# The second normalisation of a two-layer graph network: transposes and scores from fp16 halves, in another order

## The reference

```python
h = relu(layernorm(x))                              # layer 0
x = x + (adj != 0) @ (h @ W0 + b0) / deg[:, None]    # deg: column sums of adj != 0

h = relu(layernorm(x))                              # layer 1, the second normalisation
ht = (h @ W1) split into 4 heads of 512
src, dst = ht . a_src, ht . a_dst                   # one score per node and head
e = leaky_relu(src[i] + dst[j], 0.01) + adj[i, j]
x = x + mean over heads of softmax(e, over j) @ ht
```

## Time and profile before

| | us |
|---|---|
| median of three runs | 2477.36 (2476.27 to 2477.75) |
| profiled execution | 2477.34 |
| its span | 2475.5 |
| TensorE busy in the span | 2451.6 (99%) |
| VectorE, ScalarE busy | 1873.6 (76%), 1259.9 (51%) |
| layer 0 up to its last block | to 350.03 |
| last block with the second normalisation | 350.03 to 428.92 |
| hand-over to layer 1's first matmul | 428.92 to 441.94 |

### The profile page before, as it was taken

One profiled execution on the slowest core, in us unless ns is written; L12 is line 12 of the kernel. 1 busy time (PEld: TensorE's weight loads), 2 busy tenths in 40 slices (PEclk: granted clock), 3 DMA queues, 4 the chain that ended last, 5 costly groups with the idle time before them and its releaser, 6 DMA issues.

```text
span 2475.5 us, 42808 instructions
## 1 busy us (share of the span) xinstructions
PE 2451.6 (99%) x12355; PEld 1199.9 (48%) x12355; DVE 1873.6 (76%) x2575; ACT 1259.9 (51%) x1886; POOL 47.8 (2%) x44
## 2 busy tenths in 40 slices
PE   7999999999999999999999999999999999999999
PEld 4444446444444444444444444444444444444787
DVE  7788767976688676887768876687776887667786
ACT  4645546744455444554445544455445554444554
POOL 0000000000000000000000000000000000000000
PEclk9999999999999999999999999999999999999999
DMA  4276747100121001210012000121000300001000
GB/s 149 98 273 187 246 154 224 60 3 5 43 81 37 1 5 34 89 35 4 5 34 89 35 4 5 34 89 35 4 5 27 96 34 3 3 13 49 26 1 10
DMA packets 74079, 143.95 MB, mean 58 GB/s; under 512 B 4473, under 2 KB 11899, under 8 KB 72826
## 3 DMA queue, kind: packets, MB, share of 16 engines
q1 hardware_dynamic: 73978, 142.82, 18.0%
HBM read 129.11 MB, written 13.70 MB: 58 GB/s over the span
## 4 chain that ended last, share of the span: by engine, by line
PE 83%; issue 10%; DVE 5%; DMA 1%; ACT 1%; POOL 0%; DVEq 0%; POOLq 0%; ACTq 0%
PE z_ps L776 70%; PE o_ps L804 11%; DVE hl_reg L977 2%; DMA ring_reg<-adjT_in 1%; PE o_ps L1428 1%; PE c_ps L1428 1%; DVE z_reg L993 0%; DVE ao_reg L990 0%; ACT h_reg L1251 0%; DVE w_reg L1075 0%; DVE t_reg L968 0%; PE o_ps L1413 0%; ACT w_reg L1258 0%; PE c_ps L790 0%; DVE hl_reg L968 0%
## 5 line engine op out<-in xcount | busy, mean ns | idle before, releaser
L776 PE MATMUL z_ps<-hl_reg,h_reg 128*128 (+2 forms) x8712 | 1752.0, 364 | 1.3 <-DVE hl_reg L635 1.3
L776 PEld LDWEIGHTS z_ps<-hl_reg,h_reg 128*128 (+1 forms) x8712 | 852.4, 98 | 897.6 <-issue 2.3
L574 ACT ACTIVATE hl_reg<-t_reg (+2 forms) x363 | 360.7, 994 | 722.3 <-DVE t_reg L663 379.2
L635 DVE TENSOR_TENSOR hl_reg<-t_reg,hl_reg (+2 forms) x363 | 416.5, 1147 | 229.3 <-ACT hl_reg L574 226.9
L559 ACT ACTIVATE t_reg<-ring_reg,vv 128x512 f32 (+3 forms) x726 | 524.8, 770 | 66.3 <-DVE ao_reg L650 60.9
L663 DVE SCALAR_TENSOR_TENSOR t_reg<-t_reg,vv,e_reg (+3 forms) x728 | 510.5, 743 | 8.5 <-issue 8.0
L650 DVE TENSOR_TENSOR ao_reg<-ao_reg,t_reg 128x1024 f32<-128x1024 f32 (+1 forms) x336 | 383.8, 1142 | 0.0
L804 PE MATMUL o_ps<-w_reg,z_reg 128*128 128x512 f16 x1248 | 278.2, 379 | 0.9 <-DVE z_reg L679 0.9
L804 PEld LDWEIGHTS o_ps<-w_reg,z_reg 128*128 128x128 f16 x1248 | 119.8, 98 | 140.9 <-DVE z_reg L679 1.2
L679 DVE SCALAR_TENSOR_TENSOR z_reg<-z_ps,z_reg 128x512 f16<-128x512 f32 (+1 forms) x112 | 73.2, 654 | 151.5 <-ACT z_reg L586 151.5
L463 ACT ACTIVATE e_reg<-e_reg (+2 forms) x91 | 90.5, 995 | 152.7 <-DVE e_reg L474 152.7
(11 more groups left out here) (178 smaller groups left out, 1094.8 us busy)
## 6 DMA issues: line engine op xcount, KB each, us to landing
ring_reg<-adjT_in SPq DMA_DIRECT2D x78, 512.0 KB, 4.5
e_reg<-adjT_in SPq DMA_DIRECT2D x78, 512.0 KB, 3.6
ring_reg<-x_in SPq DMA_DIRECT2D x13, 512.0 KB, 4.1
x_dram<-ring_reg SPq DMA_DIRECT2D x13, 512.0 KB, 5.0
ao_reg<-x_dram SPq DMA_DIRECT2D x6, 1024.0 KB, 5.6
out_dram<-ao_reg SPq DMA_DIRECT2D x6, 1024.0 KB, 4.5
ring_reg<-c_dram SPq DMA_DIRECT2D x23, 256.0 KB, 3.3
h_reg<-x_in SPq DMA_DIRECT2D x3, 1536.0 KB, 15.8
```

The costliest lines, as they stand in the source:

```text
L574: nc.scalar.activation(hl_ring[:, g % HL_RING, 0, :, 0:W], t_ring[:, g % T_RING, :, 0:W], ACT.Copy).then_inc(hi_ready, 1)
L635: nc.vector.tensor_tensor(hl_ring[:, g % HL_RING, 1, :, 0:W], t_ring[:, g % T_RING, :, 0:W], hl_ring[:, g % HL_RING, 0, :, 0:W], ALU.subtr ...
L776: mm = nc.tensor.matmul(z_ps[:, k, 0:W], hk[hs], hl_ring[:, r, ps, u, 0:W], start=first and u == 0 and n == 0, stop=last and u == 1 and n ...
```

## The change

For all tiles but the last, the fp16 halves in `h16` are transposed instead of the fp32 stage: eight fp16 transposes per tile into the same bank, one copy of 1024 fp16 elements to `ht1_16`, and four times two matmuls with `wa16`, the two fp16 halves of `wa` side by side (16 columns). The eight columns of each half are added by VectorE at the end (`sdc`). A transpose now waits for the pair's low half. The scores of a tile come one step after the transposes of the next. Steps and maxima are placed anew. The first four pairs are loaded early into `ln1_stage` itself and are normalised there in place; the sums of eight tiles run in the last eleven turns of `awork`. The halves of tiles 20 to 22 go to `late_h`, a part of `ao_reg`, and are moved to `h16` by a DMA after the late steps, for which TensorE waits after the first 24 matmuls of layer 1. In VectorE's groups splits are put between the sums, ScalarE's order is written out, and the variances of the last group but one come ahead of the remaining splits and row maxima.

```diff
-        LN1_AT = [math.ceil(6 + 5 * m / 3) for m in range(NT - 1)]
+        LN1_AT = [math.ceil(5 + 1.9 * m) for m in range(NT - 1)]
-        LATE_MAX_AT = [4, 10, 16]
-        MR_AT = 24
+        LATE_MAX_AT = [4, 17, 27]
+        MR_AT = 36
+        SUM_G = LAST0 + 2
...
                 def transpose1(i):
-                    pe.wait_ge(st1_ready, i + 1)
+                    t = tiles1[i]
+                    if i == 0:
+                        pe.wait_ge(o_sb, o_count(NB - 1))
                     if i >= 2:
                         pe.wait_ge(tr_sb, i - 1)
-                    for k in range(KT):
-                        mm = nc.tensor.transpose(o_ps[:, i % 2, k * P:(k + 1) * P],
-                                                 ln1_stage[:, (i // 2) % 2, i % 2, k * P:(k + 1) * P], ident[:])
+                    if i < NT - 1:
+                        pe.wait_ge(st1_split, unit(i) + 1)
+                        pe.wait_ge(s_i16, 1)
+                        h = late_h[:, t - L0] if L0 <= t < L0 + 3 else h16[:, t]
+                        for s in range(2):
+                            for k in range(KT):
+                                mm = nc.tensor.transpose(o16[:, i % 2, (s * KT + k) * P:(s * KT + k + 1) * P],
+                                                         h[:, s, k * P:(k + 1) * P], ident16)
...
                 def scores(i):
...
                     for k in range(KT):
-                        mm = nc.tensor.matmul(c_ps[:, t * 2 * H:(t + 1) * 2 * H], ht1[:, i % 2, k], wa3[:, k],
-                                              start=k == 0, stop=k == KT - 1)
+                        if i < NT - 1:
+                            for s in range(2):
+                                mm = nc.tensor.matmul(c_ps[:, t * 4 * H:(t + 1) * 4 * H], ht1_16[:, i % 2, s, k],
+                                                      wa16[:, k].rearrange("p s r -> p (s r)"),
+                                                      start=k == 0 and s == 0, stop=k == KT - 1 and s == 1)
...
                         if step == LN1_AT[i]:
                             transpose1(i)
-                            if i > 0:
-                                scores(i - 1)
+                        if i > 0 and step == LN1_AT[i] + 1:
+                            scores(i - 1)
...
+                scores(NT - 3)
                 scores(NT - 2)
                 pe.wait_ge(mr_sb, 1)
                 pe.wait_ge(st1_split, 1)
...
+                def early1(n):
+
+                    if n == 0:
+                        degrees1(0, EARLY)
+                        x1_sums(0, 2)
+                    if n == 1:
+                        x1_sums(2, 4)
+                    if n == 2:
+                        variances1(0)
+                        ln_scalars(dve, *groups1[0], NG0)
+                    if n == 4:
+                        split1(0)
+                        degrees1(EARLY, 2 * EARLY)
+                    if n == 5:
+                        split1(1)
+                    if n == 8:
+                        x1_sums(4, 6)
+                    if n == 9:
+                        x1_sums(6, 8)
+                    if n == 10:
+                        variances1(1)
+                        ln_scalars(dve, *groups1[1], NG0 + 1)
...
+                dve.wait_ge(sd_ps, NT - 1)
+                for t0, t1 in ((0, L0 + 3), (L0 + 4, NT)):
+                    nc.vector.tensor_scalar(sdc3[:, t0:t1], sc_ps[:, t0:t1, 0], 1.0, None, ALU.mult).then_inc(s_sdc, 1)
+                dve.wait_ge(s_sdc, 2)
+                for t0, t1 in ((0, L0 + 3), (L0 + 4, NT)):
+                    nc.vector.tensor_tensor(sdc3[:, t0:t1], sdc3[:, t0:t1], sc_ps[:, t0:t1, 1], ALU.add).then_inc(s_sdc, 1)
                 subtract_max(dve, 0, E_PRE0)
                 dve.wait_ge(sd_ps, NT)
+                nc.vector.tensor_scalar(sdc3[:, L0 + 3], sc_ps[:, L0 + 3, 0], 1.0, None, ALU.mult).then_inc(s_sdc, 1)
+                dve.wait_ge(s_sdc, 5)
                 nc.vector.tensor_reduce(dmx[:], sd_rt, AX_X, ALU.max).then_inc(s_dmx, 1)
...
+                sp.wait_ge(a_pe, NA)
+                sp.wait_ge(st1_split, PAIRS)
+                sp.dma_start(h16[:, L0:L0 + 3], late_h).then_inc(late_in, 16)
...
             mm.then_inc(hl_free, 1)
+            pe.wait_ge(late_in, 16)
```

ScalarE's new order for a group of four tiles, with `back` the number of the tile whose transposes are copied:

```diff
+                for c in range(2, 5):
+                    relus1(c)
+                    for j in (2 * c, 2 * c + 1):
+                        relu1(2 * j)
+                        transposed1(back)
+                        relu1(2 * j + 1)
+                        high1(j)
+                        if j == 2 * c + 1:
+                            next_sqrt(c)
+                        transposed1(back + 1)
+                        back += 2
```

More of the change, by code:

```diff
@@ L331, in gnn_kernel @@
         xr_in = [sem(f"xr_in{s}") for s in range(ADJ_RING)]
+        xe_in = [sem(f"xe_in{j}") for j in range(EARLY)]
+        xe_out = [sem(f"xe_out{j}") for j in range(EARLY)]
+        late_in = sem("late_in")
+        s_i16 = sem("s_i16")
+        s_wa16 = sem("s_wa16")
+        s_sdc = sem("s_sdc")
         x1_ready = sem("x1_ready")
@@ new lines, in x1_place, with x1_tile @@
+                def x1_place(i):
+                    j = i // 2
+                    return ln1_stage[:, j % 2, i % 2] if j < EARLY else x_ring[:, (NA + j - EARLY) % ADJ_RING, i % 2]
+                def x1_tile(i):
+                    t, j = tiles1[i], i // 2
+                    if i % 2 == 0:
+                        if j < EARLY:
+                            dve.wait_ge(xe_in[j], 16)
+                        else:
+                            dve.wait_ge(xr_in[(NA + j - EARLY) % ADJ_RING], ((j - EARLY) // ADJ_RING + 1) * 16)
+                    it = t - L0
+                    if 0 <= it < IT:
+                        if it < IT - 1:
+                            dve.wait_ge(o_ready, (IT - 1) * (NB - 2) + 1 + it + 1)
+                        else:
+                            dve.wait_ge(a_pe, NA)
+                        o = acc0(NB - 1, it)
+                    else:
+                        dve.wait_ge(o_sb, o_count(order.index(t // IT)) + t % IT + 1)
+                        o = xs[:, t]
+                    nc.vector.scalar_tensor_tensor(out=x1_place(i), in0=o, scalar=rdeg[:, t:t + 1],
+                                                   in1=x1_place(i), op0=ALU.mult, op1=ALU.add).then_inc(x1_ready, 1)
@@ new lines, in x1_stats, with x1_sums, split1 @@
+                def x1_stats(i):
+                    dve.wait_ge(x1_ready, i + 1)
+                    nc.vector.bn_stats(bst3[:, tiles1[i]], x1_place(i)).then_inc(x1_bst, 1)
+                def x1_sums(i0, i1):
+                    for i in range(i0, i1):
+                        x1_tile(i)
+                    for i in range(i0, i1):
+                        x1_stats(i)
+                def split1(j):
+                    t, n = tiles1[2 * j], 2
+                    dve.wait_ge(hi1_done, j + 1)
+                    h = late_h[:, 0:2] if t == L0 else h16[:, t:t + 2]
+                    nc.vector.tensor_tensor(h[:, :, 1], ln1_stage[:, j % 2], h[:, :, 0],
+                                            ALU.subtract).then_inc(st1_split, 1)
@@ new lines, in _ @@
+                for c in (5, 6):
+                    i0 = tiles_of(c)
+                    relus1(c)
+                    relu1(i0)
+                    transposed1(back)
+                    relu1(i0 + 1)
+                    high1(i0 // 2)
+                    next_sqrt(c)
+                    transposed1(back + 1)
+                    back += 2
+                    if c == 5:
+                        max_rows()
+                transposed1(back)
+                relus1(7)
+                relu1(NT - 2)
@@ L1386, in _ @@
+                high1_one(0)
+                for i in range(back + 1, NT - 1):
+                    transposed1(i)
+                next_sqrt(7)
+                relus1(8)
+                relu1(NT - 1)
                 transposed1(NT - 1)
```

295 lines of the change are left out of this document (176 added, 119 removed).

## The result

The changed kernel takes 2465.07 us (median of five, 2464.07 to 2467.23) against 2476.43 us; the ratio is 0.9954 with a 95% interval of 0.9942 to 0.9965, 0.5% faster. 2465.2 was forecast. The profiled execution took 2466.71 us, its span is 2465.0.

A forecast was written before the change was run, and what follows sets the result against it. TensorE, busy 99% of the span, was taken as the bound. Block and hand-over terms summed to 70.6 us against 82.9, 12.3 less; minus 0.2 for the added copy, 2477.34 - 12.1 = 2465.2 us, range 2462.0 to 2471.5.

The forecast's parts named there:

- The price of the scores: TensorE, layer 0's last block: eight fp16 score matmuls take 0.25 us a tile instead of 0.81, 14.0 us for 25 tiles.
- The price of the transposes: TensorE, layer 0's last block: eight fp16 transposes at 0.056 us each, 0.45 us a tile, as before.
- The 81 ns of the Trainium skill: Rival for the fp16 transposes: sustained 81 ns each, 0.65 us a tile, gain 8.8 us, 2468.5 us; chance 0.10.
- The copy: ScalarE after each tile's transposes: 1024 fp16 elements take 0.95 us instead of 0.48, bounds 0.48 and 1.2.
- The cycle of ScalarE and VectorE: Last block, per group of four tiles: their hand-overs take 10.2 us, longer than TensorE's 9.4 by 0.8.
- Idle time in the block: TensorE's waits in layer 0's last block: 2.5 us, against 1.96 today.
- its walk: Queues followed instruction by instruction through the last block: 2.0 us of TensorE waits, raised to 2.5.
- After the last step: From the last step's end to the last tile's transposes: 5.2 us, including 1.05 us of waiting for the copy.
- The score copies: VectorE, between last scores and their maximum: one copy of eight scores adds 0.2 us; four larger ones end earlier.
- Edits costed at nothing: Early loads, stores, the weights' preparation and the late halves' DMA: all hidden, 0 us.
- TensorE's lead of thirteen pairs: Adjacency work before the last block: TensorE runs thirteen pairs of 3.45 us behind VectorE, which would absorb a late tile.
- The late DMA: Moves three tiles' halves (768 KB) after the last step; hidden before TensorE asks 18 us after it, at least 0.5 to spare.

The follow-up runs named there:

- the fill experiment: Changed kernel with the first two early loads of x three turns later and five of 14 fillers ahead of the last fp16 scores: 2463.37 us, ratio 0.9941.
- the kernel without the head start: Changed kernel with sums, scalars, ReLUs and splits of the first eight tiles run after the adjacency work's last turn: 2485.45 us beside 2476.64.

## Why the prediction was right, point by point

*The price of the scores* was the gain, as forecast. 0.205 us were measured for 0.25, near the lower bound from the row sums; over the 23 groups in the block that is 1.0 us more gain. Issuing them four times over took the whole gain away.

*The price of the transposes*: 0.445 forecast as 0.45, read off the slope between 512 and 256 columns. The 81 ns of the Trainium skill ("TensorE: Matmul & The Clock Gate", "Back-to-back issue gap") did not show: 56 ns with eight and with sixteen in a row. The same section of the Trainium skill gives N/2.4 + 2.5 ns for a single, isolated gap, which is 55.8 for N = 128 and fits the measured spacing.

*The copy*: 0.95 forecast, 0.90 measured (359.75 to 360.65 in ScalarE's timeline), of fp16 and not cheaper for its bytes. *The cycle of ScalarE and VectorE*: 10.2 us forecast per group; VectorE's rows at the same place of the cycle (the first sum behind the row maximum) in two groups:

```profile
366.96 1.41 DVE L1239 SCALAR_TENSOR_TENSOR ring_reg<-h_reg,rdeg,ring_reg 128x512 f32<-128x512 f32 x2
...
377.17 1.41 DVE L1239 SCALAR_TENSOR_TENSOR ring_reg<-h_reg,rdeg,ring_reg 128x512 f32<-128x512 f32 x2
```

They are 10.2 us apart, where TensorE's own work for four tiles is 7.6 x 0.865 + 4 x (0.445 + 0.205) = 9.2 us. That this cycle is the longer one was shown by taking work off each side.

*Idle time in the block*: the waits stand at the forecast places (0.42 ahead of the first maxima, 0.34 at the last of the maxima's transposes, 0.16 to 0.34 four times for copies). These bracketed numbers add up to 1.7 us, but they are not what the forecast's sum is made of. A bracket counts from the end of the matmul before, which the profile puts 0.16 us late (a late step is given as 1.03 us long, though the next instruction can start 0.865 us after its first); the first instruction behind a wait is a little longer too. From start to start the block's work is 44.95 + 24 x 0.445 + 23 x 0.205 + 1.4 = 61.7 us, and it took 64.72: 3.0 us of idle time where 2.5 was forecast. The kernel with the halved copy, with one wait left, took 62.28, which bears the sum out. So the 0.5 us that the forecast had added to its walk was needed, and the term was still 0.5 too small.

*After the last step*: 5.2 us forecast, 5.18 measured, with 1.07 us of waiting for the copy from start to start (0.93 in the bracket; 1.05 forecast); the last tile's ReLU was indeed not what ended last, as the fill experiment showed. *The score copies*: here a term of the sum was too small. 0.2 us was forecast and 0.54 measured up to layer 1's first matmul. The copy itself takes 0.2 (424.78 to 424.98), but the maximum over the copied scores takes 0.53 instead of 0.38 us, the differences 0.34 instead of 0.27, and the exponentials, whose scale is now read from SBUF (`wacoef`) instead of being a constant, 0.65 for two instead of 0.47 and 0.38 for the one behind them instead of 0.29:

```profile
424.78 0.17 DVE L1340 TENSOR_SCALAR ao_reg<-c_ps 128x8 f32<-128x8 f32 x1 [2.06 <-PE c_ps L1682]
424.98 0.53 DVE L1342 TENSOR_REDUCE dmx<-ao_reg 128x8 f32<-128x208 f32 x1
```

Which of these is due to SBUF as the place of the scores and which to the operand was not tried.

*Edits costed at nothing*: this step failed, though the number hardly shows it. "SyncE's queue asks for adjacency tiles four ahead of VectorE, and each is needed far later" was the reason given, with TensorE's lead of thirteen pairs as the second cover. The lead does cover TensorE's matmuls. It doesn't cover the wait ahead of pair 65, which asks for VectorE's maxima of turns 74 to 77, with VectorE only just in time: it cost 0.4 us already. Two loads ahead of pair 76 made that 1.23 to 2.68 us in the nine profiles of the changed kernel or of one whose edits lie behind that place; behind three of these nine waits TensorE's matmuls ran slower as well. The late DMA, on the other hand, is hidden: it took 11.5 us to land from 419.25, and TensorE asks for it at 436.9.

So that the number came out within 0.2 us is partly luck. The forecast was also built on 2477.34 us, while the kernel before took 2476.43 beside the result; of the gain, 12.1 us were forecast and 11.4 measured. From the last block's first step to the last tile's transposes the changed kernel took 69.9 us where 70.6 was forecast: 1.1 less for the scores, 0.1 less for the transposes, 0.5 more of idle time. The old stretch was 83.3 and not 82.9, and the score copies cost 0.3 more than forecast. Together the block and the hand-over gave 12.8 us where 12.1 was forecast. Layer 0, costed at nothing, took 2.5 of it back in the profiled execution, and less in others: by the medians the gain is those 11.4. Because of layer 0 the last step ended at 417.2 and layer 1's first matmul came at 431.6, where "near 415" and "near 429.6" stood among the signs. The waits named for ScalarE's copy, "about 2 us in the block", are 0.9 us in brackets and, with a fifth one at 388.66 that has none, 1.9 from start to start.

## What to carry to other kernels

With 128x128 fp16 weights a matmul of few columns was about four times cheaper in the queue than an fp32 one (26 ns with 16 columns, 101 with 8), but the freed time is only collected if the engines that feed it keep up; walk their cycle, hand-overs included, and compare its period with the new one. Small reductions that TensorE waits for belong where VectorE's own order has already passed them: here their place alone was worth 16 us. Before an early load is called free, look for one-off waits ahead, where the general lead doesn't count, not only at the consumer of the delayed tiles.

## What the runs showed of the hardware

A wait of about 2 us in TensorE's queue is sometimes followed by a stretch at the lower of the two clock levels. The same wait, in the same place, was 1.96 us in the first profile of the changed kernel and 1.93 us in the second. The windows of 300 to 320 us, first and second:

```profile
300.00:320.00 20.00, 18.04 (x77) 7.68 (x76) 16.97 (x26) 9.73 (x28) 0.00 (x0) 0.91 0.67 218
```

```profile
300.00:320.00 20.00, 18.07 (x84) 8.02 (x83) 17.93 (x27) 9.72 (x28) 0.00 (x0) 1.00 0.81 256
```

In the first the 12 matmuls behind it took 4.29 us, in the second 2.60: 1.7 us of difference between two executions of one kernel. In the other experiments' kernels, too, this wait ahead of pair 65 had both outcomes: with 2.08, 2.40 and 2.68 us it was followed by slower matmuls, with 1.23, 1.59, 1.64, 1.99 and again 2.08 us it was not. Nor was the wait of 1.96 us in the kernel before, nor any in the last block up to 1.71 us. All three waits of the kernel with early maxima, of 2.41, 5.07 and 4.98 us, were followed by it (granted clock 0.78, 0.79 and 0.78 over the next 7.4 to 7.9 us), and so were the two of 5.36 and 8.73 us in the kernel without the head start. What decides it near 2 us was not tried.

A kernel that avoids such waits might vary less from run to run, but the times don't show it. The one with the later loads and the new filler order has 1.05 us between its extremes, against 2.17 for the changed kernel beside it; the one with the later loads alone avoids the wait too and has 1.90.
